# Cross-attention loop: the turn of the probabilities moved from TensorE to VectorE and transfers, and the steps skewed by one more

## The reference

```python
x = x + _L0_xattn_ref(_layernorm(x), ctx_2048, mask, Wq, bq, Wk, bk, Wv, bv, Wo, qn_w, kn_w)
x = x + _L0_ffn_ref(_layernorm(x), w_router, ...)
# _L0_xattn_ref, 16 query heads of 128, 4 key heads, 128 queries and 128 keys per batch
q = _rmsnorm((hidden_states @ Wq + bq), qn_w); k = _rmsnorm(context @ Wk + bk, kn_w); v = context @ Wv + bv
probs = softmax(q k^T / sqrt(128) + mask)
out = (probs v) @ Wo
# _L0_ffn_ref: picks 16 of 128 tokens per batch by a router score; attention and an MLP on the picks only
```

## Time and profile before

| what | value |
|---|---|
| median of 3 runs | 873.27 us (870.92 to 874.57) |
| the profiled execution's own time | 873.5 us |
| its span | 871.6 us |
| TensorE (PE) busy | 820.1 us, 94% of the span |
| VectorE (DVE) busy | 578.2 us, 66% |
| ScalarE (ACT) busy | 472.4 us, 54% |
| GpSimd (POOL) busy | 464.4 us, 53% |
| mean granted TensorE clock | 0.980 |

### The profile page before, as it was taken

The page is one execution under the profiler, slowest core; times in us unless marked ns, Lnnn a source line. Parts: engine busy times, 40 slices in busy tenths (PEclk is TensorE's granted clock), DMA queues, the critical chain, the costliest instruction groups (busy, mean ns, idle before and its releaser), DMA issues. The chain is left out here.

```text
span 871.6 us, 14174 instructions
## 1 busy us (share of the span) xinstructions
PE 820.1 (94%) x4216; PEld 684.2 (78%) x4216; DVE 578.2 (66%) x1049; ACT 472.4 (54%) x1620; POOL 464.4 (53%) x485
## 2 busy tenths in 40 slices
PE   6999988999999999999999999999987799878997
PEld 5888766888888888888888888888865577766786
DVE  4455456677777777777777777777677587763512
ACT  4555454565565565665655655655653265553431
POOL 2333353564554655654655555555557196544880
PEclk9999998999999999999999999999997799998999
DMA  7566654111111111111011021121024654302520
GB/s 233 201 205 200 198 172 133 37 49 60 36 48 59 38 48 53 35 56 49 34 61 47 27 70 39 34 72 36 12 91 161 207 193 165 138 31 90 193 97 24
DMA packets 49287, 81.37 MB, mean 93 GB/s; under 512 B 4144, under 2 KB 12464, under 8 KB 49264
## 3 DMA queue, kind: packets, MB, share of 16 engines
q1 hardware_dynamic: 48688, 79.25, 27.3%
q0 software_dynamic: 576, 1.84, 0.6%
HBM read 63.77 MB, written 17.30 MB: 93 GB/s over the span
## 5 line engine op out<-in xcount | busy, mean ns | idle before, releaser
L938 ACT ACTIVATE sq_junk<-q_row 128x128 bf16<-128x128 f32 x256 | 76.0, 298 | 151.3 <-DVE q_row L1261 151.3
L845 POOL TENSOR_TENSOR wp_lo<-raw,wp_hi 128x2048 fp32r<-128x2048 f32 (+1 forms) x24 | 104.9, 4384 | 46.1 <-ACT wp_hi L910 45.9
L1008 ACT ACTIVATE p_row<-s_row,neg_max 128x128 f32<-128x128 f32 x256 | 99.9, 391 | 36.7 <-DVE neg_max L1282 36.7
L1661 PE MATMUL b_y<-wo_hi,oT_hi 128*128 128x512 f32 x256 | 108.2, 423 | 1.0 <-DVE oT_lo L1186 1.0
L777 POOL TENSOR_TENSOR p_row<-p_row,p_inv 128x512 f32<-128x512 f32 x64 | 66.6, 1041 | 69.5 <-DVE p_inv L1291 69.5
L1661 PE MATMUL b_q<-wq_hi,xT_hi 128*128 128x512 f32 x248 | 102.7, 414 | 0.0
L1663 PE MATMUL b_y<-wo_hi,oT_lo 128*128 128x512 f32 x256 | 102.0, 398 | 0.0
L1662 PE MATMUL b_y<-wo_lo,oT_hi 128*128 128x512 f32 x256 | 101.8, 398 | 0.0
L1663 PE MATMUL b_q<-wq_hi,xT_lo 128*128 128x512 f32 x248 | 97.4, 393 | 0.0
L1662 PE MATMUL b_q<-wq_lo,xT_hi 128*128 128x512 f32 x248 | 96.8, 391 | 0.0
L735 POOL TENSOR_TENSOR q_rs<-q_ss,eps_head 128x4 f32<-128x4 f32 x64 | 12.9, 202 | 143.0 <-ACT sq_junk L938 143.0
(11 more groups left out here) (301 smaller groups left out, 2273.4 us busy)
## 6 DMA issues: line engine op xcount, KB each, us to landing
cx<-in_ctx_dram SPq DMA_DIRECT2D x16, 256.0 KB, 2.7
raw<-in_L_xattn_Wq_dram SPq DMA_DIRECT2D x16, 256.0 KB, 2.8
raw<-in_L_xattn_Wo_dram SPq DMA_DIRECT2D x16, 256.0 KB, 3.2
v_store<-v_out SPq DMA_DIRECT2D x16, 256.0 KB, 3.4
k_store<-k_out SPq DMA_DIRECT2D x16, 256.0 KB, 2.0
xr<-in_x_dram SPq DMA_DIRECT2D x16, 256.0 KB, 2.7
k_raw<-k_store SPq DMA_DIRECT2D x16, 256.0 KB, 2.6
v_raw<-v_store SPq DMA_DIRECT2D x16, 256.0 KB, 2.8
```

What stands on the lines that cost most here:

```text
L845: pool.tensor_tensor(wp_lo[n % NSLOT][:, part, :], raw[RAW_OF[n]][:, part, :], wp_hi[n % NSLOT][:, part, :].bitcast(fp32), ALU.subtract).t ...
L938: sq = act.activation(sq_junk[:, h, :], q_row[:, h, :], ACT.Square, accum_out=q_ss[:, h:h + 1])
L1008: e = act.activation(p_row[:, h, :], s_row[:, h, :], ACT.Exp, bias=neg_max[:, h:h + 1], accum_out=p_sum[:, h:h + 1])
L1661: pe.matmul(dst, left[0], right[0], start=start, stop=False)
```

## The change

The probabilities of a step (128 queries by four heads of 128 keys) are no longer turned by TensorE. VectorE turns each 32x32 block in place in the grid of blocks (p_turn, STREAM_TRANSPOSE, into p_tr), and four transfers from SBUF to SBUF, one for each group of 32 queries (load_p), spread the blocks over the partitions into one of two buffers (pT_in). Partition 4d + j then holds key 32j + d; load_v loads v's rows in the same order. p_high now reads SBUF, and p_low moves from VectorE to GpSimd. The buffers lie in raw[1], whose first FFN weights are loaded at the end of the last batch and not after the first. Every stage behind the scores runs one step later (exps, p_norm, p_turn one behind the scores, mix two, add_y three), and the order inside a step is new on all engines. Steps 62 and 63 are still turned on TensorE, after the loop. The core of the diff (the lines that begin with # name the engine; the rest of it moves the once-a-batch pieces, the drain after the loop and the waits that go with them):

```diff
+        p_tr = raw[1][:, 0, :].rearrange("p (j h s) -> p j h s", j=4, h=QUAD)
+        pT_in = [raw[1][:, 1 + i, :].rearrange("p (i h s) -> p i h s", i=4, h=QUAD) for i in range(2)]
...
+        DMA_TURNED = STEPS - 2
...
+        def by_head(tile_):
+            return tile_[:].rearrange("p (h i s) -> p h i s", h=QUAD, i=4)
...
             def load_v(b):
-                sp.dma_start(v_raw[:], v_store[bass.ds(b * P, P), :]).then_inc(v_loaded, 16)
+                sp.dma_start(v_raw[:], v_store[bass.ds(b * P, P), :].rearrange("(j d) n -> d j n", j=4)
+                             ).then_inc(v_loaded, 16)
...
+            def load_p(t, par):
+                sp.wait_ge(p_turned, t + 1)
+                for i in range(4):
+                    sp.dma_start(pT_in[par][:, i].rearrange("p h s -> p (h s)"),
+                                 p_tr[32 * i:32 * i + 32].rearrange("d j h s -> d j (h s)")
+                                 ).then_inc(pT_loaded, 16)
...
# GpSimd
+            def p_low(t, par):
+                pool.wait_ge(pT_hi_done, t + 1)
+                pool.tensor_tensor(by_head(pT_lo), pT_in[par].rearrange("p i h s -> p h i s"),
+                                   by_head(pT_hi).bitcast(fp32), ALU.subtract).then_inc(pT_lo_done, 1)
...
-                    p_norm(t)
+                    if not (first and i == 0):
+                        p_norm(t - 1)
+                    if not (first and i < 2):
+                        p_low(t - 2, i % 2)
+                    if not (first and i < NQUAD - 1) and not (last and i == NQUAD - 1):
+                        q_norm(t + 1)
...
# ScalarE
-            def p_high(t):
+            def p_high(t, par):
+                act.wait_ge(pT_loaded, 64 * (t + 1))
+                wait(act, mixed, t)
+                copy(by_head(pT_hi), pT_in[par].rearrange("p i h s -> p h i s")).then_inc(pT_hi_done, 1)
+
+            def last_p_high(t):
                 act.wait_ge(p_turned, t + 1)
...
-                    q_high(t)
-                    if not (last and i == NQUAD - 1):
+                    if not (first and i < NQUAD - 1):
+                        o_high(t - 3)
...
                     if not (first and i == 0):
-                        p_high(t - 1)
+                        exps(t - 1, last and i == NQUAD - 1)
+                    if not (first and i < 2):
+                        p_high(t - 2, i % 2)
+                    if not (first and i < NQUAD - 1) and not (last and i == NQUAD - 1):
+                        q_high(t)
...
# VectorE
-            def p_low(t):
+            def p_turn(t):
+                dve.wait_ge(p_normed, t + 1)
+
+                wait(dve, pT_loaded, 64 * t)
+                dve.transpose(p_tr, p_row[:].rearrange("p h (j d) -> p j h d", j=4)).then_inc(p_turned, 1)
+
+            def last_p_low(t):
...
# TensorE
                     if not (first and i < NQUAD - 1) and not (last and i == NQUAD - 1):
                         project_q(t + 1, b if i < NQUAD - 1 else b + 1, (i + 1) % NQUAD)
-                    score_quad(t, b, i)
...
+                    turn_q(t)
...
+                    if not (first and i < NQUAD - 1):
+                        add_y(t - 3, b if i == NQUAD - 1 else b - 1, (i + 1) % NQUAD)
+                    if i == NQUAD - 1 and not first and not last:
+                        spread_scores(b - 1, b + 2)
+                    score_quad(t, b, i)
                     if not (first and i < 2):
-                        add_y(t - 2, b if i >= 2 else b - 1, (i - 2) % NQUAD)
-                    if not (first and i == 0):
-                        mix(t - 1, b if i >= 1 else b - 1, (i - 1) % NQUAD)
+                        mix(t - 2, b if i >= 2 else b - 1, (i + 2) % NQUAD)
```

More of the change, by code:

```diff
@@ L612, in store_rows @@
                 sp.dma_start(out_rows[bass.ds(b * S, S), :], x1[:]).then_inc(base_stored, 16)
-            def attend(b, first, last):
[L615 to L632, removed]
@@ new lines, in attend @@
+            def attend(b, first, last):
+                for i in range(NQUAD):
+                    t = NQUAD * b + i
+                    if i == 0 and not first and not last:
+                        sp.wait_ge(x_normed, b + 1)
+                        load_x(b + 1)
+                    if not (first and i == 0) and not (last and i == NQUAD - 1):
+                        load_p(t - 1, (i - 1) % 2)
+                    if i == 0 and not last:
+                        sp.wait_ge(kT_hi_done, b + 1)
+                        sp.wait_ge(kT_lo_done, b + 1)
+                        load_k(b + 1)
+                    if i == 1 and first:
+                        keys_over(sp)
+                        spread(wr_row[:], w_router).then_inc(wr_loaded, 16)
+                        sp.wait_ge(kv_w_hi, DC)
+                        sp.wait_ge(kv_w_lo, DC)
+                        sp.dma_start(raw[0][:], PIECES[0]).then_inc(raw_loaded[0], 16)
+                    if i == 2:
+                        sp.wait_ge(v_hi_done, b + 1)
+                        sp.wait_ge(v_lo_done, b + 1)
+                        if not last:
+                            load_v(b + 1)
+                    if i == NQUAD - 1 and not first:
+                        sp.wait_ge(x1_made, b)
+                        sp.dma_start(x_res[:], x_rows[bass.ds(b * S, S), :]).then_inc(res_loaded, 16)
+                        if last:
+                            last_loads()
+                        store_rows(b - 1)
@@ L652, in load_piece @@
                 sp.dma_start(raw[RAW_OF[n]][:], PIECES[n]).then_inc(raw_loaded[RAW_OF[n]], 16)
[L655 to L672, removed]
             load_piece(2)
@@ L857, in _ @@
             row_rsqrt(0)
+            p_norm(STEPS - 1)
             split_low(0)
@@ L1001, in o_high, with exps @@
                 copy(oT_hi[:], b_o[:]).then_inc(oT_hi_done, 1)
-            def exps(t):
+            def exps(t, by_row=False):
                 act.wait_ge(s_maxed, t + 1)
@@ L1048, in _ @@
             row_squares(0, h_sel[0][:])
-            p_high(STEPS - 1)
+            o_high(STEPS - 3)
+            last_p_high(STEPS - 2)
+            exps(STEPS - 1, True)
+            o_high(STEPS - 2)
+            last_p_high(STEPS - 1)
             def split_high(n):
@@ L1377, in attend @@
                     t = NQUAD * b + i
[L1378 to L1383, removed]
+                    if first and i == NQUAD - 1:
+                        keys_over(dve)
+                    if not (first and i < NQUAD - 1):
+                        o_low(t - 3)
+                    if i == 1 and not last:
+                        x_norm(b + 1)
+                    if i == NQUAD - 1 and not first and not last:
+                        norm_out(b - 1)
+                    if (first and i < NQUAD - 1) or (last and i == NQUAD - 1):
+                        q_low(t)
+                    if not (first and i == 0):
+                        p_invert(t - 1)
+                    if last and i == NQUAD - 1:
+                        norm_out(b - 1)
+                    if first and i == 1:
+                        q_bias(3, 3)
+                    if not (first and i < NQUAD - 1) and not (last and i == NQUAD - 1):
+                        q_bias(t + 1, (i + 1) % NQUAD)
+                    if not (first and i < NQUAD - 1) and not (last and i == NQUAD - 1):
+                        q_low(t)
+                    if i == 2 and not last:
+                        x_low(b + 1)
+                    if first and i == 1:
+                        dve.wait_ge(w_hi, 2 * NB)
+                        dve.wait_ge(w_lo, 2 * NB)
                     if i == 0 and not last:
@@ L1387, in attend @@
                         dve.wait_ge(x_stats, b + 2)
-                    if not (first and i == 0):
-                        q_low(t)
+                    if not (first and i == 0) and not (last and i == NQUAD - 1):
+                        p_turn(t - 1)
                     if i == 0 and not last:
                         x_moments(b + 1)
[L1392 to L1396, removed]
+                    if last and i == 0:
+                        dve.wait_ge(kT_hi_done, NB)
+                        dve.wait_ge(kT_lo_done, NB)
+                        select_rows(0)
+                    if last and i == 1:
+                        number_rows(0)
+                    if i == 2 and not first:
+                        add_residual(b - 1)
+                        dve.wait_ge(x1_stats, b)
+                    if i == NQUAD - 1 and not first and not last:
+                        rank(b - 1)
                     s_mask(t)
+                    if i == 2 and not first:
+                        x1_moments(b - 1)
                     s_sum(t)
+                    if last and i == NQUAD - 1:
+                        o_low(STEPS - 3)
                     s_max(t)
@@ L1401, in attend @@
                         q_bias(2, 2, b_y)
[L1402 to L1425, removed]
             attend(0, True, False)
@@ L1431, in _ @@
```

(13 more changed lines are left out.)

92 lines of the change are left out of this document (48 added, 44 removed).

## The result

The changed kernel takes 859.15 us (median of four runs, 857.3 to 860.1) beside 872.1 us for the kernel before (870.1 to 874.6): ratio 0.985, 95% interval 0.982 to 0.988. It is faster (the forecast had drawn that line at 868.9) and inside the range of 843 to 872, but by 13 us where 23 were forecast. The profiled execution took 860.1 us, its span 858.4; before these were 873.5 and 871.6.

A forecast was written before the change was run, and what follows sets the result against it. TensorE was taken to bound the attention loop: 873.5 - 26.7 (62 turns removed) + 2.2 (spread_scores) + 1.4 (late x and such) = 850.4, so 850 us; own range 843 to 857, 8-in-10 range 843 to 872.

The forecast's parts named there:

- a slow p_turn: Rival on VectorE: p_turn up to 1.49 us makes the vector chain the bound; 857 to 870 us, chance 0.17.
- signs of being right: In the loop: TensorE 99 to 100% busy, batch 31.3 to 31.5 us, p_turn near 0.7, last landing 3.5 later, p_high not waiting.
- the third rival: p's transfers land late, so p_high on ScalarE waits, then q_high and the scores; 908 us at 4.3 landing, chance 0.16.
- dearer spread_scores: TensorE, once a batch: spread_scores pays its own switch, at most 0.16 us, 2.2 us in the 14 loop batches.
- The second rival: VectorE's p_turn above 1.1 us, TensorE waiting for q_low, the vector chain the bound; 857 to 870 us, chance 0.17.
- p_high, p_low: Splits of p: p_high on ScalarE from SBUF at 0.63 us, p_low moved to GpSimd at 1.30 us.
- Landing 2.0: Each SBUF-to-SBUF transfer of p lands after 2.0 us, by the k_store row; 2.7 by the HBM load row.
- Issue 0.50: SyncE issues p's four 64 KB transfers per step at 0.50 us from issue to issue.
- L: Time from p_turn's end to the last landing of p's transfers: 3.5 us, or 4.2 by the other row.
- the slack: What the softmax chain has to spare under TensorE: 1.3 us a batch (30.0 against 31.36), 0.95 a step.
- late by some tenths in step 0: load_x on SyncE waits behind the store of x1; small delay within 0.95 us slack, allowed 0.1 a batch, 1.4 us.
- Fill and drain: Start and end of the attention loop: waits get other causes, one more step is open; nothing taken, 3 us either way.

The follow-up runs named there:

- x_early: Changed kernel with the load of x issued in step 2 of the batch before, behind p's four transfers: 845.08 us, ratio 0.970.
- x_early_turns: x_early plus four unread identity transpositions on TensorE per step between scores and mix, in the 14 loop batches: 869.93 us, ratio 0.998.
- x_early_one: x_early with one plain 256 KB transfer per step in place of four of 64 KB (result differs): 845.49 us.
- two_transfers: Changed kernel with two of the four transfers per step left out, x still late: 848.15 us, ratio 0.973.

## Why the prediction was right in kind and short in size

- **The range.** 859.15 lies in the 843 to 872 that were to hold 8 in 10, but not in the 843 to 857 of the forecast itself: what reaches up to 870 stood for a slow p_turn, and that did not come. The range held by luck. Of the signs of being right only p_turn came. TensorE was 98.3% busy and not 99 to 100, the batch 32.10 us and not 31.3 to 31.5, the last landing 4.1 us behind p_turn and not 3.5, and ScalarE waited 0.34 us per batch ahead of p_high, ended by a DMA, which was to show the third rival. x_early has the same transfers and not that wait, so it came from x.
- **TensorE bounds the loop, and its relief is worth the full price.** Right. The forecast had 0.43 us per turn and a dearer spread_scores, 31.36 us a batch; x_early has 31.04. The turn was worth 0.45 (batches of 32.84 and 31.04, over four), and no dearer spread_scores shows: before and x_early_turns, with the same work, differ by 0.08 us a batch the other way.
- **p_turn** at 0.69: it took 0.70 in the median of 62, 0.71 at most. The second rival didn't come. By the Trainium skill's "VectorE: DVE Perf Modes", section "The three transpose paths", the estimate was 1.24 us, four times a figure for one tile in bf16; the trace, in fp32, disagrees, and the measurement decides.
- **p_high, p_low**: forecast 0.63 and 1.30, measured 0.62 and 1.30.
- **The transfers.** Landing 2.0, measured 2.1. That was partly luck: the forecast took k_store as the row for a source in SBUF, and the page of the kernel before has v_store, out of SBUF too, at 3.4. Issue 0.50, taken from two loads in a row; measured 2.51 / 4 = 0.63. L was 3.5, with 4.2 as the other end; from 384.81 to 388.92 it is 4.1. The prediction said that 4.2 would be 0.48 us too long but inside the slack, and with x in time it is: x_early pays nothing. The Trainium skill's "DMA: Bandwidth & Descriptors", "Rules for kernel authors", asks to coalesce small transfers; x_early_one agrees as to L (from p_turn's end at 374.83 to landing, 0.03 + 2.3 = 2.3 us against 4.1), and no time hung on it.
- **The step that failed: load_x**, "late by some tenths in step 0", at 0.1 us a batch. It was 1.43 us late and cost 0.93 to 1.06 a batch (32.10 less 31.04). The place was right, the size wasn't, and the "some tenths" had not been worked out from rows. Three things were missed. The load landed in 3.2 us, not the 2.7 of the earlier trace rows; in two_transfers, where it landed in 2.6 and p came sooner too, the cost was 0.08. The slack in that step was 0.72, not 0.95, since TensorE's interval there is 7.61 and not the mean of 7.84. And p's transfers start late with x: their 4.1 us no longer fit ahead of p_high, 0.34 more. (The forecast named only base_rows as what holds the store of x1; p's issues, x_res and h_store hold it as long, but either alone does, so this changed no number.) It is 14 x 0.96 = 13 us too little allowed; the cheaper TensorE batch gives 4.5 of it back, and 8.9 of the 10 missing are so found in the loop.
- **Fill and drain**, 0 within 3: 1.2 us gained from the first scores to step 4 and 1.2 after step 60, where six of the 62 turns (2.6 us) lie outside the 14 batches. The 2.6 us by which the first scores came later in this profile lie within what the same code differs by. The FFN's 1.7 us, not forecast, I didn't follow up.

## What to carry to other kernels

When work moves to a queue, every later transfer of that queue moves too: ask of each one who stands behind its consumer, and give it an early place in the order (x's load could go out half a batch sooner at no cost). Where a slack is shared, take the slack of that very step and add up all delays that draw on it: the transfers, harmless with x in time, cost 0.34 us behind a late x. When the bound engine falls below 100% busy, tabulate its intervals by step: the one that grew tells where to look.

## Not expected of the hardware

- Transfers inside SBUF of 64 KB (128 pieces of 512 bytes) issue at 0.60 to 0.63 us each in a row of four, whether or not they change the partition, against 0.48 for one of 256 KB. Those that change it landed in 2.1 to 2.2 us.
- The 256 KB store of x1 landed in 3.3 us in the changed kernel and in 2.0 in the kernel before, in two_transfers and in x_early_one. Where it took 2.0 it left at least 1.5 us after the issue ahead of it had ended; in the changed kernel 0.26 us after. The load of x behind it took 3.2 and, in two_transfers, 2.6. That four transfers ahead are enough for this is not shown: in x_early the load of x leaves right behind four of them and landed in 2.7.
- Turning 512 fp32 elements per partition in 32x32 blocks on VectorE takes 0.70 us, as long as an addition of the same size.
